# The last block's queries in two halves: even tiles in the first half of the last attention period, odd tiles in the second

## The chip, the core and the metric

The program runs on one core of one Trainium2 chip. The metric is the device time of one execution in microseconds (us); lower is better. Four engines do the arithmetic: TensorE (PE, matrix multiplies; its weight loads are shown as PEld), VectorE (DVE), ScalarE (ACT) and GpSimd (POOL). SyncE (SP) issues the DMA transfers. Each engine runs its own list of instructions strictly in order, and waits for semaphores that others raise.

## What is computed

The input `x` is (4, 64, 64, 64) float32, the output (4, 4096, 64). The three layers, cut to what matters here:

```python
# token layer: a 3x3 filter whose taps are computed per pixel
y = relu(batchnorm(conv1_w @ x)); wdyn = conv2_w @ y + conv2_b
h = sum_k(patches_k(x) * wdyn_k).reshape(b, 4096, 64)
# attention over 4096 tokens, one head of width 64
n = layernorm(h); Q, K, V = n @ Wq + bq, n @ Wk + bk, n @ Wv + bv
h = h + softmax(Q @ K.T / 8) @ V
# feed-forward: each token goes to the best of 32 experts with 16 hidden units each
n = layernorm(h); e = argmax(n @ router_w.T + router_b)
h = h + relu(relu(n @ W1[e] + b1[e]) @ W2[e] + b2[e])
```

## The kernel before

**Blocks.** The 4 x 4096 tokens are worked on in 16 blocks of 1024 queries (`BLOCKS`, numbered 0 to 15); four blocks make one image. A block has 8 tiles of 128 tokens (`BT`), laid out for TensorE as two halves of 512 columns. The keys of an image are 32 tiles, taken as 16 pairs (`PAIRS`).

**Periods.** The program is a list of periods. Period n has 16 groups g = 0 to 15, and in each of them TensorE computes the scores of one pair of key tiles against all 1024 queries of block n (`usual_score`, line 689) and then adds the previous group's exponentials times the keys into the sum `z_ps` (`usual_weigh`, `into_z`, line 700). ScalarE takes the exponentials in between (line 912) into a ring of four buffers. Period 16 has no attention left: it is the tail, in which only the stages of the last block run.

**Stages.** Between score and weighing a group may have "fills", small stages of other blocks, named `name@block`. For a finished block they are, in order: `z` (VectorE adds the two halves of `z_ps` into `z_sb`, lines 1109 and 1111; TensorE may not begin the next sum in `z_ps` before, semaphore `z_copied`); `pz` (TensorE projects to values, line 626; VectorE divides by the softmax sum, adds the residual and normalises, lines 1175 to 1181 and 1010 to 1038, result `y_block`); `yt` (turned by TensorE, line 547, copied to `y_t` by ScalarE, line 889); `lg` (router logits, line 635, copied by ScalarE, line 897; VectorE picks the expert, lines 1053 to 1063, result `onehot`); `ot` (turned, line 547, copied to `onehot_t`, line 900); `hid0` to `hid3` (first expert layer, line 656); `o2` (second layer, lines 663 and 671; its two halves added into `o2_sb`, lines 863 and 1191); `fin` (turned back, line 679; VectorE adds, line 1197, and SP stores the block, line 362).

**Experts.** In blocks 3 to 13 (`CHOSEN_BY_DMA`) the choice of the expert is spread by DMA and VectorE applies it (line 1143). In the others TensorE adds a mask of large negative numbers first (line 652, bf16) and ScalarE takes the relu (line 904); for the last block ScalarE and VectorE take half of it each (lines 904 and 1149, semaphore `upper_hidden`).

**Places.** A fill's result goes to a place in PSUM. The usual one is `both` (place 0), of which there is one, so a fill waits until the fill before it has been read. Once attention is over, the banks of `scores` and `z_ps` are free as well: table `AT_THE_END` spreads the last stages over them (places 7 and 8 are the two banks pairs of `scores`, 9 is `z_ps`).

**What sets the order.** The tables of groups: `usual_groups(n)` puts, in period n, the stages of block n-1 (`pz` at group 2, `yt` 5, `lg` 6, `ot` 8, `hid0` to `hid3` 12 to 15, `o2` 16, `fin` at group 1 of the period after). For block 14 the last two are missing from period 15, because `last_groups` puts `hid0@14` to `hid3@14` and `o2@14` into the tail, behind `pz@15`. Every engine walks through the same tables. In blocks 0 and 1 (n < 2) the attention goes another way, in halves; that part is not touched.

Of the kernel before, what the change touches and what calls it, by code (L numbers as in the profile page):

```python
# [8 lines left out]
ALU = mybir.AluOpType  # L9
# [8 lines left out]
D = W  # L18
HH = 2
# [49 lines left out]
CHOSEN_BY_DMA = range(3, BLOCKS - 2)  # L69
USUAL, FIRST_TAP, TAP_PLACES = 0, 1, 6  # L70
# [10 lines left out]
def at(i, names):  # L81
    return [f"{n}@{i}" for n in names.split()] if 0 <= i < BLOCKS else []
# [120 lines left out]
def vit_block_kernel(nc, x, once, kept, out):  # L203
# [6 lines left out]
    with ExitStack() as ctx:  # L210
# [64 lines left out]
        centred, squares = tap_product[:, 0], tap_product[:, 1]  # L275
# [1056 lines left out]
```

## Time and profile before

| | us |
|---|---|
| three timed runs | 1128.85, 1130.23, 1126.38 (median 1128.85) |
| the profiled execution, its own time | 1131.35 |
| its span in the trace | 1129.3 |
| TensorE busy | 1091.9 (97% of the span) |
| ScalarE busy | 584.1 (52%) |
| VectorE busy | 545.5 (48%) |
| last weighing (line 700) to the end of the span | 35.6 |

The page of the profile gives the busy share of each engine in 40 slices of 28 us. TensorE stands at 9 (90% or more) in all slices except the first and the last. The row of its granted clock stands at 9 (full speed) in most slices and at 8 in the last. The timeline lists instructions in order of time, merged, with the idle time of the engine before them and what released it; a matmul of float32 counts as two instructions in the trace (and as one in the listings of the order below). Four 64x64 matmuls run side by side, so the starts of a row's instructions lie closer together than one of them lasts.

### The profile page before, as it was taken

How to read it: one execution, taken by the hardware profiler on the slowest of the kernel's cores; microseconds unless marked ns; L12 is line 12 of the kernel's file. 1: busy time of each engine (PE TensorE's matmuls, PEld its weight loads, DVE VectorE, ACT ScalarE, POOL GpSimd, SP SyncE). 2: the span in 40 equal slices, each digit the busy share in tenths (PEclk: the TensorE clock that was granted, in tenths of full speed). 3: DMA queues.
4: the chain of work that ended last, by engine and by line, in shares of the span. 5: the costliest groups of instructions: out<-in, count | busy, mean ns of one | idle time of the engine just before them, and what ended most of it. 6: DMA issues, size and time to landing. Idle time of an engine off the chain costs nothing.

```text
span 1129.3 us, 28862 instructions
## 1 busy us (share of the span) xinstructions
PE 1091.9 (97%) x12458; PEld 520.4 (46%) x12458; DVE 545.5 (48%) x1145; ACT 584.1 (52%) x654; POOL 10.7 (1%) x35
## 2 busy tenths in 40 slices
PE   6699999999999999999999999999999999999995
PEld 2233333445444554445544455544545555555542
DVE  6788766428056472645637264553523131412323
ACT  2356666555555464555546455464545455454552
POOL 3000000000000000000000000000000000000000
PEclk9989999999999999999999999999999999999998
DMA  5645612122025131232412123140100101010000
GB/s 152 144 112 127 150 38 61 34 45 61 16 70 117 39 87 23 69 77 61 86 39 82 26 69 78 40 105 10 42 11 11 41 11 41 11 42 10 2 1 20
DMA packets 22385, 63.86 MB, mean 57 GB/s; under 512 B 3550, under 2 KB 7454, under 8 KB 21868
## 3 DMA queue, kind: packets, MB, share of 16 engines
q1 hardware_dynamic: 22252, 61.93, 22.8%
q8 instruction: 102, 1.67, 0.7%
q14 instruction: 31, 0.25, 0.1%
HBM read 53.31 MB, written 5.47 MB: 52 GB/s over the span
## 4 chain that ended last, share of the span: by engine, by line
PE 89%; DVE 5%; issue 2%; DMA 1%; ACT 1%; DVEq 1%; SPq 0%; ACTq 0%
PE z_ps L700 37%; PE scores L689 35%; PE both L656 4%; PE both L671 4%; PE both L547 2%; DMA filter_ring<-filters 1%; PE both L679 1%; PE both L595 1%; PE both L585 1%; PE both L616 1%; DVEq L1004 1%; PE both L626 1%; PE both L635 0%; ACT probs L912 0%; PE both L663 0%
## 5 line engine op out<-in xcount | busy, mean ns | idle before, releaser
L912 ACT ACTIVATE probs<-scores 128x1024 f32<-128x1024 f32 x504 | 488.7, 1021 | 462.2 <-PE scores L689 462.2
L689 PE MATMUL scores<-g_t,keys_t 64*64 64x512 f32 x4096 | 511.0, 593 | 3.0 <-ACT g_t L891 1.2
L700 PE MATMUL z_ps<-probs,keys 64*64 64x512 f32 x4096 | 505.8, 591 | 0.7 <-issue 0.7
L689 PEld LDWEIGHTS scores<-g_t,keys_t 64*64 64x64 f32 x4096 | 206.7, 134 | 242.3 <-issue 235.3
L700 PEld LDWEIGHTS z_ps<-probs,keys 64*64 64x64 f32 x4096 | 193.4, 133 | 193.5 <-issue 183.6
L1143 DVE SCALAR_TENSOR_TENSOR hidden<-both,chosen 128x1024 f32<-128x1024 f32 x44 | 53.9, 1224 | 198.9 <-PE both L656 193.9
L1079 DVE TENSOR_TENSOR hres<-hres,tap_product 128x504 f32<-128x504 f32 (+1 forms) x128 | 88.8, 694 | 10.5
L1074 DVE SCALAR_TENSOR_TENSOR tap_product<-filter_ring,w,xin 128x504 f32<-128x504 f32 (+1 forms) x120 | 89.0, 742 | 6.2 <-DMA filter_ring<-filters 2.9
L656 PE MATMUL both<-y_t,w 64*64 64x512 f32 x464 | 63.4, 597 | 0.0
L671 PE MATMUL both<-hidden,w 64*64 64x512 f32 x448 | 56.6, 592 | 0.0
L1187 DVE COPY o_sb<-both 128x512 f32<-128x512 f32 x14 | 9.7, 691 | 82.9 <-PE both L671 82.9
L1109 DVE COPY z_sb<-z_ps 128x512 f32<-128x512 f32 x14 | 9.7, 692 | 69.6 <-PE z_ps L700 69.6
L656 PEld LDWEIGHTS both<-y_t,w 64*64 64x64 f32 x464 | 22.6, 134 | 24.5 <-issue 23.9
L1053 DVE TENSOR_REDUCE stat<-logits 128x8 f32<-128x256 f32 x16 | 6.7, 419 | 55.4 <-ACT logits L897 55.4
L671 PEld LDWEIGHTS both<-hidden,w 64*64 64x64 f32 x448 | 23.8, 133 | 20.7 <-issue 19.8
L1175 DVE RECIPROCAL stat<-both 128x8 f32<-128x8 f32 x16 | 3.3, 208 | 57.4 <-PE both L626 57.4
L1029 DVE TENSOR_TENSOR tap_product<-tap_product 128x512 f32<-128x512 f32 x32 | 22.2, 692 | 2.7 <-issue 0.4
L1031 DVE TENSOR_REDUCE stat<-tap_product 128x8 f32<-128x512 f32 x32 | 22.0, 686 | 2.3
L547 PE MATMUL both<-w,keys 64*64 64x64 f32 x512 | 11.8, 232 | 10.5 <-DVE keys L1038 10.3
L547 PEld LDWEIGHTS both<-w,keys 64*64 64x64 f32 x512 | 11.3, 145 | 21.7 <-issue 21.7
L1015 DVE SCALAR_TENSOR_TENSOR stat<-stat 128x8 f32<-128x8 f32 x96 | 16.1, 167 | 7.9 <-issue 0.9
L1019 DVE SCALAR_TENSOR_TENSOR stat<-stat 128x8 f32<-128x8 f32 x96 | 16.1, 167 | 7.8 <-issue 0.9
(138 smaller groups left out, 552.8 us busy)
## 6 DMA issues: line engine op xcount, KB each, us to landing
filter_ring<-filters SPq DMA_DIRECT2D x90, 384.0 KB, 5.2
chosen<-choices SPq DMA_DIRECT2D x44, 256.0 KB
out_dram<-out_sb SPq DMA_DIRECT2D x32, 128.0 KB, 2.6
xin<-x_dram SPq DMA_DIRECT2D x6, 528.0 KB, 9.1
g_t<-g_t SPq DMA_DIRECT2D x24, 128.0 KB, 5.6
hidden<-once_dram SPq DMA_DIRECT2D x1, 930.0 KB, 12.5
choices<-onehot_t SPq DMA_DIRECT2D x22, 32.0 KB, 1.6
hidden<-once_dram SPq DMA_DIRECT2D x1, 576.0 KB, 4.6
```

Of the source, the lines that this page charges most:

```text
L547: last = T.matmul(both[rows_of(a), h, j * 64:(j + 1) * 64], tiles[2 * j + a][rows_of(h)], ident[rows_of(h), rows_of(h)], start=True, stop= ...
L656: last = T.matmul(mine[rows_of(c), r, :], w1[rows_of(r), cols[c]], y_t[rows_of(r), :], start=i in CHOSEN_BY_DMA, stop=True)
L671: last = T.matmul(mine[rows_of(r), h, :], w2[rows_of(h), f, :], hidden[rows_of(h), f, r, :], start=(f == 0 and h != r), stop=(f == FT - 1))
L689: last = T.matmul(scores[rows_of(h), c, r * 512:(r + 1) * 512], keys_t[rows_of(r), i // NQ % 2, k * 128 + 64 * h:k * 128 + 64 * h + 64], g ...
L700: last = T.matmul(z_ps[rows_of(c), h, :], keys[rows_of(h), i // NQ % 2, 2 * k + r, :], probs[rows_of(h), (2 * g + c) % RING, r * 512:(r + ...
L912: A.activation(probs[:, unit % RING, :], scores[:, c, :], ACT.Exp, scale=first_scale[:, 0:1] if n == 0 and g <= ASKED else SCALE).then_inc ...
L1015: V.scalar_tensor_tensor(half, dst, -0.5, dst, ALU.mult, ALU.mult)
L1029: V.tensor_tensor(squares[:, :, :], centred[:, :, :], centred[:, :, :], ALU.mult)
L1031: V.reduce_sum(total, squares[:, :, :], AX_X)
L1074: product = V.scalar_tensor_tensor(dst, flt, keep["b2c"][:, t:t + 1], pix, ALU.add, ALU.mult)
L1079: V.tensor_tensor(mine[:, :, lo:hi], mine[:, :, lo:hi], dst, ALU.add)
L1143: V.scalar_tensor_tensor(hidden[:, f, :, :], place[k][:, :, :], 0.0, chosen[:, f, :, :], ALU.max, ALU.mult).then_inc(drained[k], 1)
```

## The change

The last block (15) becomes two parts. Part `EVEN` (number 15) holds its tiles 0, 2, 4, 6, part `ODD` (number 16) its tiles 1, 3, 5, 7, 512 queries each. In period 15 the first 8 groups work on all 32 key tiles for the even queries, the second 8 groups on all of them for the odd queries: a group takes two pairs of key tiles against one half of the queries, where it took one pair against both halves. Number and shape of the score and weighing matmuls stay.

The stages of `EVEN` then run inside period 15, from its group 8 on (`z`, `pz`, `yt`, `lg`, `ot`), and its `hid`, `o2`, `fin` in the tail; those of `ODD` all run in the tail. Block 14's `hid0` to `hid3` and `o2` move from the tail into period 15, its `fin` stands in the tail. Stages of a part are half as wide (256 columns in place of 512), `pz` apart, whose TensorE part keeps its size. Each part is stored by itself, 64 partitions x 4 tiles of 256 bytes in each of two DMAs, in place of 64 partitions x 2048 bytes.

```diff
-AT_THE_END = {f"{name}@{BLOCKS - 2}": k for name, k in (("hid0", 7), ("hid1", 8), ("hid2", 7), ("hid3", 8), ("o2", 9))}
-AT_THE_END |= {f"{name}@{BLOCKS - 1}": k for name, k in (("hid1", 7), ("hid2", 8), ("o2", 9))}
+AT_THE_END = {f"fin@{EVEN - 1}": 7, f"fin@{EVEN}": 9}
+AT_THE_END |= {f"{name}@{EVEN}": k for name, k in (("hid0", 8), ("hid1", 9), ("hid2", 8), ("hid3", 9), ("o2", 8))}
+AT_THE_END |= {f"{name}@{ODD}": k for name, k in (("hid1", 7), ("hid2", 8), ("o2", 9))}
...
-def attention(n, g):
-
-    if n > 1:
-        return n, g
-    return g // HALF, n * HALF + g % HALF
+def attention(n, g, c):
+
+    if n < 2:
+        return g // HALF, n * HALF + g % HALF, c
+    if n == BLOCKS - 1:
+        return n, g % HALF * 2 + c, g // HALF
+    return n, g, c
...
+def halved_groups():
+
+    m = EVEN - 1
+    return merged(usual_groups(BLOCKS - 1),
+                  {HALF: at(EVEN, "z"), 9: at(m, "hid0"), 10: at(EVEN, "pz"), 11: at(m, "hid1"), 12: at(m, "hid2"),
+                   13: [*at(m, "hid3"), *at(EVEN, "yt")], 14: at(EVEN, "lg"), 15: at(m, "o2"), 16: at(EVEN, "ot")})
...
-    m = BLOCKS - 1
-    return merged({-1: at(m, "z"), 2: at(m, "pz"), 3: at(m - 1, "hid0 hid1 hid2 hid3 o2"), 5: at(m, "yt"), 6: at(m, "lg"),
-                   7: at(m - 1, "fin"), 8: at(m, "ot"), 9: at(m, "hid0 hid1 hid2 hid3"), 15: at(m, "o2"),
-                   16: at(m, "fin")})
+    return merged({-1: at(ODD, "z"), 1: at(EVEN - 1, "fin"), 2: at(ODD, "pz"), 3: at(EVEN, "hid0 hid1 hid2 hid3 o2"),
+                   5: at(ODD, "yt"), 6: at(ODD, "lg"), 7: at(EVEN, "fin"), 8: at(ODD, "ot"),
+                   9: at(ODD, "hid0 hid1 hid2 hid3"), 15: at(ODD, "o2"), 16: at(ODD, "fin")})
...
+                    if m < EVEN:
+                        rows, mine = (v.rearrange("c t w -> c (t w)") for v in (rows, mine))
+                    else:
+                        rows = rows.rearrange("c (j a) w -> c a j w", a=2)[:, m - EVEN]
+                    sp.dma_start(rows, mine).then_inc(out_stored[m % 2], 16)
...
-                        pe.wait_ge(z_copied, n)
+                        pe.wait_ge(z_copied, n + (g > 0))
...
+            def half_block(i, sums, done):
+
+                tiles = residual(EVEN).rearrange("p (j a) w -> p a j w", a=2)[:, i - EVEN]
+                whole = tap_product[:, :, :, :].rearrange("p k t w -> p (k t w)")[:, 0:BT // 2 * 65]
+                whole = whole.rearrange("p (j w) -> p j w", w=65)
+                rs, mine = stat[:, 4, 0:BT // 2], h2[:, i % 2, 0:BT // 2, :]
+                settle()
+                V.tensor_copy(whole, sums[:, 0])
+                settle()
+                V.tensor_tensor(whole, whole, sums[:, 1], ALU.add).then_inc(done, 1)
+                settle()
+                V.reciprocal(rs, whole[:, :, D])
+                settle()
+                V.tensor_tensor(mine, whole[:, :, 0:D], wide(rs, D), ALU.mult)
+                settle()
+                V.tensor_tensor(mine, mine, tiles, ALU.add)
+                settle()
+                normalise(mine)
+                write_normalised(y_block[:, 0:BT // 2, :]).then_inc(y_ready, 1)
```

**Order on TensorE at the end of period 15, before:** attention runs undisturbed to its last two weighings (x16), and `pz@15` and `hid0@14` follow.

```order
L689 MATMUL scores<-g_t,keys_t 64x512 x8
L700 MATMUL z_ps<-probs,keys 64x512 x16
L626 MATMUL both<-wv_w,z_sb 64x65 x16
L652 MATMUL scores<-onehot_t,mask_w 64x512 x4
L656 MATMUL scores<-y_t,w 64x512 x4
```

**The same place after** (groups 13 to 16; line 726 is the score, 737 the weighing, 687 and 692 `hid3@14`, 581 `yt@EVEN` and then `ot@EVEN`, 668 `lg@EVEN`, 700 and 708 `o2@14`):

```order
L687 MATMUL both<-onehot_t,mask_w 64x512 x4
L692 MATMUL both<-y_t,w 64x512 x4
L581 MATMUL both<-w,y_block 64x64 x8
L737 MATMUL z_ps<-probs,keys 64x512 x8
L726 MATMUL scores<-g_t,keys_t 64x512 x8
L668 MATMUL both<-router_w,y_t 64x32 x8
L737 MATMUL z_ps<-probs,keys 64x512 x8
L726 MATMUL scores<-g_t,keys_t 64x512 x8
L700 MATMUL both<-onehot_t,b_parts 64x512 x4
L708 MATMUL both<-hidden,w 64x512 x16
L737 MATMUL z_ps<-probs,keys 64x512 x8
L581 MATMUL both<-ident_bf,onehot 64x64 x8
```

Block 14's expert layers and four small stages of `EVEN` now stand between score and weighing of period 15, and `hid3@14` and `yt@EVEN` stand next to each other in the same place `both`.

**Order on TensorE in the tail, before** (from the last of `hid3@14`: `o2@14`, `yt@15`, `lg@15`, `fin@14`, `ot@15`, `hid0@15`):

```order
L656 MATMUL scores<-y_t,w 64x512 x4
L663 MATMUL z_ps<-onehot_t,b_parts 64x512 x4
L671 MATMUL z_ps<-hidden,w 64x512 x16
L547 MATMUL both<-w,y_block 64x64 x16
L635 MATMUL both<-router_w,y_t 64x32 x16
L679 MATMUL both<-w,o_sb 64x64 x16
L547 MATMUL both<-ident_bf,onehot 64x64 x16
L652 MATMUL both<-onehot_t,mask_w 64x512 x4
L656 MATMUL both<-y_t,w 64x512 x4
```

**The same place after** (from the last of `hid3@EVEN`: `o2@EVEN`, `yt@ODD`, `lg@ODD`, `fin@EVEN`, `ot@ODD`, `hid0@ODD`):

```order
L692 MATMUL z_ps<-y_t,w 64x256 x4
L700 MATMUL scores<-onehot_t,b_parts 64x256 x4
L708 MATMUL scores<-hidden,w 64x256 x16
L581 MATMUL both<-w,y_block 64x64 x8
L668 MATMUL both<-router_w,y_t 64x32 x8
L716 MATMUL z_ps<-w,o_sb 64x64 x8
L581 MATMUL both<-ident_bf,onehot 64x64 x8
L687 MATMUL both<-onehot_t,mask_w 64x256 x4
L692 MATMUL both<-y_t,w 64x256 x4
```

The same stages in the same order, each at half its columns or half its count; `fin` now has a place of its own (`z_ps`), so `ot` need not wait until VectorE has read it.

**Order on VectorE between the last sum and the normalising, before:**

```order
L1109 COPY z_sb<-z_ps 128x512
L1111 TENSOR_TENSOR z_sb<-z_sb,z_ps 128x512
L1175 RECIPROCAL stat<-both 128x8
L1178 TENSOR_TENSOR h<-both,stat 128x4x64 x2
L1181 TENSOR_TENSOR h<-h,hres 128x512
L1025 TENSOR_REDUCE stat<-h 128x8
```

**After, for `ODD`** (line 1265 is `fin@14`):

```order
L1171 COPY z_sb<-z_ps 128x512
L1173 TENSOR_TENSOR z_sb<-z_sb,z_ps 128x512
L1265 SCALAR_TENSOR_TENSOR out_sb<-scores,h 128x4x64 x2
L1130 COPY tap_product<-both 128x260
L1132 TENSOR_TENSOR tap_product<-tap_product,both 128x260
L1134 RECIPROCAL stat<-tap_product 128x4
L1136 TENSOR_TENSOR h<-tap_product,stat 128x256
L1138 TENSOR_TENSOR h<-h,hres 128x256
L1065 TENSOR_REDUCE stat<-h 128x4
```

A copy and a sum are new (the two halves of the keys meet only here), the two multiplies became one, the widths are halved, and `fin@14` stands ahead.

## Rows read from the trace of the kernel before

**Rows 1.** Timeline, TensorE, period 15: start us, us, engine, line, operation, count.
```profile
1042.10 1.99 PE L689 MATMUL scores<-g_t,keys_t 64*64 64x512 f32 x16
...
1046.01 1.98 PE L689 MATMUL scores<-g_t,keys_t 64*64 64x512 f32 x16
...
1049.44 1.98 PE L689 MATMUL scores<-g_t,keys_t 64*64 64x512 f32 x16
```

**Rows 2.** Timeline, TensorE, stage o2@13 and the score behind it.
```profile
1030.96 0.38 PE L663 MATMUL both<-onehot_t,b_parts 64*64 64x512 bf16 x1
...
1034.45 2.30 PE L689 MATMUL scores<-g_t,keys_t 64*64 64x512 f32 x16
```

**Rows 3.** Timeline, TensorE, tail; in brackets idle time before and releaser.
```profile
1095.83 0.43 PE L652 MATMUL scores<-onehot_t,mask_w 64*64 64x512 bf16 x4
...
1096.91 0.42 PE L652 MATMUL scores<-onehot_t,mask_w 64*64 64x512 bf16 x4
...
1104.80 0.69 PE L547 MATMUL both<-w,y_block 64*64 64x64 f32 x32 [0.34 <-DVE y_block L1038]
...
1110.88 0.43 PE L547 MATMUL both<-ident_bf,onehot 64*64 64x64 bf16 x16 [2.75 <-DVE out_sb L1197]
1112.09 0.64 PE L652 MATMUL both<-onehot_t,mask_w 64*64 64x512 bf16 x4 [0.79 <-ACT onehot_t L900]
```

**Rows 4.** Timeline, VectorE, tail.
```profile
1093.75 0.69 DVE L1109 COPY z_sb<-z_ps 128x512 f32<-128x512 f32 x1 [30.83 <-PE z_ps L700]
...
1096.10 0.21 DVE L1175 RECIPROCAL stat<-both 128x8 f32<-128x8 f32 x1 [0.90 <-PE both L626]
...
1097.23 0.69 DVE L1181 TENSOR_TENSOR h<-h,hres 128x512 f32<-128x512 f32 x1
1097.99 0.69 DVE L1025 TENSOR_REDUCE stat<-h 128x8 f32<-128x512 f32 x1
...
1101.05 0.17 DVE L1033 TENSOR_SCALAR stat<-stat 128x8 f32<-128x8 f32 x1
...
1103.97 0.68 DVE L1038 TENSOR_TENSOR y_block<-tap_product,stat 128x504 f32<-128x504 f32 x1
...
1107.41 0.42 DVE L1053 TENSOR_REDUCE stat<-logits 128x8 f32<-128x256 f32 x1 [1.50 <-ACT logits L897]
1107.91 0.42 DVE L1055 TENSOR_TENSOR pick<-logits,stat 128x256 f32<-128x256 f32 x1
...
1124.66 0.76 DVE L1197 SCALAR_TENSOR_TENSOR out_sb<-both,h 128x256 f32<-128x256 f32 x2 [0.90 <-PE both L679]
```

**Rows 5.** Timeline, ScalarE, period 15 and tail.
```profile
1054.03 1.94 ACT L912 ACTIVATE probs<-scores 128x1024 f32<-128x1024 f32 x2 [1.49 <-PE scores L689]
1055.86 0.59 ACT L889 COPY y_t<-both 128x512 f32<-128x512 f32 x1
...
1097.17 2.10 ACT L904 ACTIVATE hidden<-scores 128x1024 f32<-128x1024 f32 x2 [5.78 <-PE scores L656]
...
1107.01 0.37 ACT L897 COPY logits<-both 128x256 f32<-128x256 f32 x1 [0.87 <-PE both L635]
...
1122.39 0.59 ACT L863 COPY o_sb<-z_ps 128x512 f32<-128x512 f32 x1 [3.27 <-PE z_ps L671]
```

**Rows 6.** Windows: stretch, length, busy per engine, TensorE's granted clock, DMA share, GB/s.
```profile
64.00:65.00 1.00, 1.00 (x12) 0.26 (x8) 0.91 (x2) 0.84 (x1) 0.00 (x0) 0.70 0.20 37
...
1109.00:1110.00 1.00, 0.00 (x0) 0.00 (x0) 0.93 (x3) 0.00 (x0) 0.00 (x0) 0.54 0.00 0
...
1115.00:1116.00 1.00, 1.00 (x8) 0.21 (x4) 0.19 (x1) 0.10 (x1) 0.00 (x0) 0.54 0.00 0
```

**Rows 7.** Timeline, TensorE, the earlier stretch at half clock.
```profile
58.69 3.69 PE L689 MATMUL scores<-g_t,keys_t 64*64 64x512 f32 x16 [0.69 <-ACT keys_t L887]
```

**Rows 8.** DMAs: landing of the 32 block stores (line 362); page, the filter loads' median.
```profile
DMA to landing us min/median/max: 2.3/2.6/3.6
...
filter_ring<-filters SPq DMA_DIRECT2D x90, 384.0 KB, 5.2
```

More of the change, by code:

```diff
@@ L432, in _ @@
             copy_queries(NQ)
-            for n in range(1, BLOCKS + 2):
+            for n in range(1, PARTS + 2):
                 if n > 1 and n % NQ == 1 and n // NQ + 2 < B:
@@ L542, in turn @@
             def turn(tiles, ident=ident):
-                for j in range(BT // 2):
+                for j in range(len(tiles) // 2):
                     for h in range(2):
@@ L631, in fill @@
                     wait_drained(f"yt@{i}")
-                    for j in range(BT // 2):
+                    for j in range(half_tiles(i)):
                         for r in range(2):
@@ L640, in fill @@
                     pe.wait_ge(onehot_ready, i + 1)
-                    last = turn([onehot[:, t, :, :].rearrange("p u e -> p (u e)") for t in range(BT)], ident_bf)
+                    last = turn([onehot[:, t, :, :].rearrange("p u e -> p (u e)") for t in range(2 * half_tiles(i))],
+                                ident_bf)
                     last.then_inc(done, 1)
@@ L645, in fill @@
                     wait_drained(f"ot@{i}")
-                    if i == BLOCKS - 1 and f == FT - 1:
+                    if i == ODD and f == FT - 1:
                         pe.wait_ge(upper_hidden, 1)
                     cols = [slice(f * 128 + 64 * c, f * 128 + 64 * c + 64) for c in range(2)]
+                    tokens = slice(0, width(i))
                     for r in range(2):
@@ L675, in fill @@
                     wait_drained(f"o2@{i}")
-                    for j in range(4):
+                    for j in range(half_tiles(i)):
                         for r in range(2):
                             for h in range(2):
-                                last = T.matmul(both[rows_of(h), r, j * 64:(j + 1) * 64],
+                                last = T.matmul(mine[rows_of(h), r, j * 64:(j + 1) * 64],
                                                 o2_sb[rows_of(r), j * 128 + h * 64:j * 128 + h * 64 + 64],
@@ L859, in drain @@
                     A.copy(a_w[:, :], z_ps[:, 1, 0:128]).then_inc(a_ready, 1)
-                if name == "o2" and i >= BLOCKS - 2:
+                if name == "o2" and i >= EVEN - 1:
                     k = places.of[full]
                     act.wait_ge(filled[k], places.nth[full])
-                    A.copy(o2_sb[:, :], place[k][:, 0, :]).then_inc(lower_copied, 1)
+                    A.copy(o2_sb[:, 0:width(i)], place[k][:, 0, 0:width(i)]).then_inc(lower_copied, 1)
                 if name.startswith(NONE) or not name.startswith(MINE):
@@ L888, in drain @@
                 elif name == "yt":
-                    A.copy(in_order(y_t[:, :]), turned).then_inc(done, 1)
+                    A.copy(in_order(y_t[:, 0:width(i)]), turned).then_inc(done, 1)
                 elif name == "g" and i < NQ:
@@ L1020, in rsqrt @@
                     settle()
-            total, var, scratch, rstd = (stat[:, k, :] for k in range(4))
             def normalise(src):
+                n = src.shape[1]
+                total, var, scratch, rstd = (stat[:, k, 0:n] for k in range(4))
+                centred, squares = (tap_product[:, k, 0:n] for k in range(2))
                 V.reduce_sum(total, src, AX_X)
@@ L1145, in drain @@
                     return
-                if name.startswith("hid") and i == BLOCKS - 1:
+                if name.startswith("hid") and i == ODD:
                     f, k = int(name[3:]), places.of[full]
                     dve.wait_ge(filled[k], places.nth[full])
-                    V.tensor_scalar(hidden[:, f, 1, :], place[k][:, 1, :], 0.0, None, ALU.max).then_inc(upper_hidden, 1)
+                    V.tensor_scalar(hidden[:, f, 1, 0:width(i)], place[k][:, 1, 0:width(i)], 0.0, None,
+                                    ALU.max).then_inc(upper_hidden, 1)
                     return
```

113 lines of the change are left out of this document (66 added, 47 removed).

## The prediction

> **What bounds the kernel now.** I read the page first: TensorE is busy for 97% of the span and has no free slice between the first and the last, so an instruction added to a period costs its full length, and only the ends hold idle time. Then the timeline of TensorE. In period 15 a group without a stage takes 1049.44 - 1046.01 = 3.43 us from score to score, without a gap [rows 1]. Then the tail, engine by engine [rows 3 to 5]: VectorE picks up the last sum at 1093.75 and the span ends at 1129.3, 35.55 us later. It is one chain that goes from engine to engine: VectorE makes `y_block` (to 1103.97 + 0.68 = 1104.65), and TensorE uses that time for `hid@14` and `o2@14`, which it leaves just before `yt@15` starts at 1104.80 after 0.34 us of idleness [rows 3, 4]. Both therefore end at about the same time. From there to the end everything lies on the path. The windows show TensorE's granted clock fall from 2.4 to 1.2 GHz inside 1109 to 1110 and rise inside 1115 to 1116 [rows 6].
>
> **What the period gains: about 10.3 us.** (1) `hid0@14` to `hid3@14`: one is 1096.91 - 1095.83 = 1.08 us with its mask [rows 3], four are 4.3. (2) `o2@14`: the same stage of block 13 takes 1034.45 - 1030.96 = 3.49 [rows 2]. (3) `pz@EVEN` keeps its size on TensorE: a group with `pz` is 1046.01 - 1042.10 = 3.91 us, so 0.48 more than an empty one [rows 1]. `yt` and `lg` have the same count of matmuls at full width and half the count here, 0.24 each; `ot`, bf16, 0.1. Together 1.06. (4) A wait is new. `yt@EVEN` stands behind `hid3@14`, in the same group and the same place `both`, and ScalarE reads `hid3@14` only behind the group's two exponentials. ScalarE's pair starts 1.16 us after the score does (1054.03 against a score start at 1046.01 + 2 x 3.43 = 1052.87) and what follows it starts 1.83 later (1055.86) [rows 1, 5], so 2.99 after the score's start; the relu of 1024 columns is half of 2.10, and 0.14 passes until TensorE goes on (y_block's end at 1104.65 to 1104.80): 4.18. TensorE is done with `hid3` at 1.72 + 1.08 = 2.80 (score, stage). It stands for 1.38 us, and the weighing, the next scores and all that follows stand with it. (5) `ot@EVEN` waits until VectorE has added `o2@14` in `both`. ScalarE's copy (0.59) and VectorE's sum (0.69) with their hand-overs take about as long as the weighing between them (1.72): 0.1. Sum 4.3 + 3.49 + 1.06 + 1.38 + 0.1 = 10.3; the last sum is ready at 1104.05.
>
> **What costs nothing there.** The new `z@EVEN`: TensorE may start the odd queries' sum only after VectorE's 1.5 us of `z`. Between the two weighings stand a score (1.72) and `hid0@14` (1.08) [rows 1, 3], 2.8 against about 1.8 with hand-overs; without `hid0` there it would be 0.1 us. VectorE is free then, its row of 1093.75 says idle for 30.83 us [rows 4]. The single place `both` between `hid0`, `pz`, `hid1`, `hid2`: each next stage stands a whole group later (3.4 us), its reader needs 1.05 behind the exponentials. Had yt stood in group 14, (4) would be gone too. The score matmuls keep number and shape. SP issues nothing new in the period.
>
> **What the tail loses.** Widths halve, fixed costs stay. From start to start VectorE needs 1097.99 - 1097.23 = 0.76 for 512 elements and 1107.91 - 1107.41 = 0.50 for 256; 12 small ones take 1103.97 - 1101.05 = 2.92 [rows 4]. By the same slope 128 elements are 0.36.
> - `z` and `pz`: 1096.10 - 1093.75 = 2.35, unchanged. `fin@14` (0.76) is taken while `pz` runs.
> - to `y_block`: 8 steps of 256 (the new copy and sum among them) 4.0, reciprocal 0.26, small ones 2.92, the last 0.42: 7.6 (before 1104.65 - 1096.10 = 8.55). `hid@EVEN` and `o2@EVEN`, half of 4.3 + 3.49 = 3.9 plus some waits for ScalarE's two places, end at about 7 and are hidden; if that cover were gone, they would cost 3.9.
> - to `ot`: before 1110.88 - 1104.65 = 6.23 [rows 3, 4], of which 0.72 is `fin@14` on VectorE in front of `ot` (the releaser of `ot@15`); it now has its own place. The two matmul stages 0.69 to 0.45 each, ScalarE 0.59 to 0.37 and 0.37 to 0.27 [rows 5], picks 4 x 0.50 to 4 x 0.36, `onehot` 0.76 to 0.5: 4.1.
> - `ot` to `hid0`: 1112.09 - 1110.88 = 1.21 becomes 0.85.
> - `hid` and `o2` of the last part: before 1122.39 - 1112.09 = 10.3 [rows 3, 5]. At full clock half of it is 2.15 + 1.75 and about 0.35 until the result: 4.25. The clock fell at 1109.08 (0.92 us of that window at half) and rose at 1115.92, 3.8 us after `hid0@15` began; at 60 us it rose at 64.6, 5.9 after the dense work of 58.69 [rows 6, 7]. Half of this time is lost. Taking the middle, 4.9: 2.45. Together 6.7.
> - to the last result: before 1124.66 + 0.76 - 1122.39 = 3.03; ScalarE, VectorE twice and a transpose narrower by 0.22 + 0.27 + 0.26 + 0.23: 2.05.
> - the store: before 1129.3 - 1125.42 = 3.9. Half the bytes, but 256 pieces of 256 bytes in place of 64 of 2048. The nearest row is the same store, landing in 2.3 to 3.6, median 2.6; the farthest in this direction the filter loads with 192 pieces, 5.2 [rows 8]. So -0.3 to +2.6; I take +0.3, near the store's own row, since 64 KB is little: 4.2.
> Sum 2.35 + 7.6 + 4.1 + 0.85 + 6.7 + 2.05 + 4.2 = 27.85, which is 7.7 less than 35.55.
>
> The net is 10.3 - 7.7 = +2.6 us. Why halving the tail's work does not pay: of the 7.8 us of `hid@14` and `o2@14` nearly all was hidden below VectorE's chain, and in the period nothing hides it. The trace of before ends at 1129.3, so after it 1131.9; the profiled execution (1131.35) lies 2.5 above the median of the runs, so I put the difference on the median: 1128.85 + 2.6 = 1131.4.
>
> **A rule against the store.** The profile's 32 stores all write pieces of 2048 bytes, and no row prices smaller ones to memory [rows 8]. The Trainium skill (DMA: Bandwidth & Descriptors, Specifications) says that full rate wants at least 512 bytes per piece and that below this the DMA engine reads, modifies and writes. No run here shows it. The rival "small pieces" has its price from the rows alone.
>
> **Rivals.** A measurement of this kernel tells 0.3% (3.4 us) from no change.
> - *The clock stays low to the end* (slower). TensorE has less to do between `o2@EVEN` and `hid0@ODD` than before: 7 us with four half-sized bursts. If the clock falls earlier, those bursts take up to 0.2 longer each (0.6), and if it does not rise before `o2@ODD` is over, all of 4.25 is doubled but for the hand-over: 3.9 in place of 2.45 lost. Sum +4.65: 1133.5. It decides when the rise comes later than about 6.5 us after `hid0@ODD`. For it: 5.9 in rows 6 and 7. Against: 3.8 in the tail itself. 0.20.
> - *Small pieces.* The last store lands like the filter loads, 5.2 in place of 2.6: +2.3 on the forecast, 1133.7. 0.08.
> - *The clock does not fall.* Idle stretches on TensorE are shorter than the 2.8 us before `ot@15`; the loss of 2.45 goes: +0.15, 1129.0. Against: less work in all than before, and it fell then. 0.10.
> - *The halves don't separate*: the choice for `EVEN` is not there when TensorE reaches `ot@EVEN`, which stands in front of the last weighing. VectorE has it about 5 us before by my count (`lg` two groups ahead, pick 2 us). If missed, each us is paid in full; 2 us give 1133.4. 0.03.
> - *The period takes less*, because the added stages find gaps that the modelled matmul ends hide, by 6 us or more: below 1125.5. TensorE's 3.43 us per group is 32 instructions at 0.107 without a gap, so hardly. 0.05.
>
> **How the numbers follow.** Forecast 1131.4 with 0.54. The range takes in the clock that does not fall at its lower end (1129.0, less 0.8 for the spread of the runs) and both slower rivals at the upper (1133.7 and a little): 1128.2 to 1134.2. Slower by over 0.3% begins at 1132.2: the two or three slower rivals give 0.31. Faster: 0.05. Within: 0.64.
>
> **What would show it.** In the profile after: the last sum's copy on VectorE at about 1104; one idle stretch of TensorE of 1.3 us in front of `yt@EVEN`, released by ScalarE's relu; `y_block` 7.6 us after `pz@ODD`; TensorE idle about 3 us before `yt@ODD`; half clock over `hid@ODD`. I am wrong if the copy comes well before 1103 (the period is cheaper) or if from there to the end it is less than 26 or more than 30 us.

## The result and the profile after

| | before | after |
|---|---|---|
| median of twelve runs, us | 1128.97 | 1133.32 |
| lowest, highest | 1126.32, 1131.52 | 1130.77, 1134.44 |
| ratio, 95% interval | | 1.003 [1.0021, 1.004] |
| the profiled execution, its own time | 1131.35 | 1132.14 |
| its span in the trace | 1129.3 | 1130.1 |

The changed kernel is slower: by 4.35 us between the medians, by 3.4 us as a ratio. The forecast was 1131.4 with a range of 1128.2 to 1134.2, so the time lies inside the range and 1.9 above the forecast, and the effect lies on the 0.3% line that was to part "no change" from "slower". Both kernels were measured once more (y1 and y2 below), which gave 1.0021 [1.0012, 1.003] for the changed one and 0.999 [0.9978, 1.0002] for the old one. Over both measurements the change costs about 2.9 us.

Two marks make the traces comparable. **M** is the start of TensorE's second score group behind `o2@13` (the group after the one at 1034.45 in [rows 2]), 1037.89 before and 1037.29 after. Up to M both kernels issue instructions of the same kind, shape and order. **Z** is the start of VectorE's last copy of the sum, 1093.75 before [rows 4]. Z - M is what period 15 and its neighbourhood take, span - Z is the tail.

The timeline of TensorE around the score at M, and at the place where period 15 of the changed kernel differs most (start us, us, engine, line, operation, count; in brackets idle time before and releaser):

```profile
1037.29 2.30 PE L726 MATMUL scores<-g_t,keys_t 64*64 64x512 f32 x16
...
1086.26 0.46 PE L687 MATMUL both<-onehot_t,mask_w 64*64 64x512 bf16 x4
1086.47 1.10 PE L692 MATMUL both<-y_t,w 64*64 64x512 f32 x8
1088.69 0.46 PE L581 MATMUL both<-w,y_block 64*64 64x64 f32 x16 [1.11 <-ACT hidden L942]
1088.97 1.90 PE L737 MATMUL z_ps<-probs,keys 64*64 64x512 f32 x16
```

The first two rows after the dots are `hid3@14`, the third is `yt@EVEN`, the last is the weighing behind it. TensorE stands idle in front of `yt@EVEN` for 1.11 us, until ScalarE has read `hid3@14`. ScalarE's timeline shows why it read so late, behind the two exponentials of the group:

```profile
1085.68 1.94 ACT L951 ACTIVATE probs<-scores 128x1024 f32<-128x1024 f32 x2 [1.55 <-PE scores L726]
1087.61 1.02 ACT L942 ACTIVATE hidden<-both 128x1024 f32<-128x1024 f32 x1
1089.22 0.37 ACT L927 COPY y_t<-both 128x256 f32<-128x256 f32 x1 [0.58 <-PE both L581]
```

The tail on VectorE (the rows that answer to [rows 4]):

```profile
1103.71 0.69 DVE L1171 COPY z_sb<-z_ps 128x512 f32<-128x512 f32 x1 [2.15 <-PE z_ps L737]
...
1106.13 0.43 DVE L1130 COPY tap_product<-both 128x260 f32<-128x260 f32 x1 [0.30 <-PE both L659]
...
1113.26 0.42 DVE L1079 TENSOR_TENSOR y_block<-tap_product,stat 128x252 f32<-128x252 f32 x1
...
1126.37 0.49 DVE L1265 SCALAR_TENSOR_TENSOR out_sb<-both,h 128x128 f32<-128x128 f32 x2 [0.66 <-PE both L716]
```

and on TensorE (to [rows 3]), the last four rows being `yt@ODD`, `ot@ODD`, `hid0@ODD` and the transpose of `fin@ODD`:

```profile
1108.96 1.89 PE L708 MATMUL scores<-hidden,w 64*64 64x256 f32 x30
1113.83 0.46 PE L581 MATMUL both<-w,y_block 64*64 64x64 f32 x16 [2.98 <-DVE y_block L1079]
...
1117.75 0.32 PE L581 MATMUL both<-ident_bf,onehot 64*64 64x64 bf16 x8 [2.10 <-DVE onehot L1105]
1118.64 0.43 PE L687 MATMUL both<-onehot_t,mask_w 64*64 64x256 bf16 x4 [0.56 <-ACT onehot_t L938]
...
1125.85 0.46 PE L716 MATMUL both<-w,o_sb 64*64 64x64 f32 x16 [1.11 <-DVE o_sb L1257]
```

VectorE now needs 1113.26 + 0.42 - 1103.71 = 9.97 us to `y_block`, before 10.90 [rows 4]. In those 10 us TensorE has less to do than before and goes idle for 2.98 us, where it was idle for 0.34 [rows 3]. ScalarE's last relevant row is the copy at 1124.81 that ends `o2@ODD`:

```profile
1124.81 0.37 ACT L900 COPY o_sb<-z_ps 128x256 f32<-128x256 f32 x1 [1.56 <-PE z_ps L708]
```

The windows over the tail (columns as in [rows 6]) show where TensorE's granted clock falls from 2.4 to 1.2 GHz and where it comes back:

```profile
1115.00:1116.00 1.00, 0.66 (x32) 0.51 (x30) 0.29 (x1) 0.27 (x1) 0.00 (x0) 0.76 0.08 16
1116.00:1117.00 1.00, 0.00 (x0) 0.00 (x0) 0.84 (x3) 0.00 (x0) 0.00 (x0) 0.50 0.00 0
...
1122.00:1123.00 1.00, 1.00 (x26) 0.80 (x22) 0.56 (x2) 0.52 (x2) 0.00 (x0) 0.83 0.00 0
```

A mean clock of 0.76 over one microsecond is 0.52 us at full and 0.48 us at half, so the clock fell at about 1115.5; 0.83 means in the same way that it rose at about 1122.3. Nearly all of `hid@ODD` therefore runs at half clock, and `o2@ODD` at full clock.

Put together, period and tail of the two kernels in two profiled executions each:

| | M | Z | Z - M | tail | Z - M + tail |
|---|---|---|---|---|---|
| before | 1037.89 | 1093.75 | 55.86 | 35.55 | 91.41 |
| before again (y2) | 1036.70 | 1092.56 | 55.86 | 34.84 | 90.70 |
| after | 1037.29 | 1103.71 | 66.42 | 26.39 | 92.81 |
| after again (y1) | 1037.50 | 1103.92 | 66.42 | 27.58 | 94.00 |

Z - M is 10.56 longer in both pairs, the tail 8.2 shorter on average, so the net is +2.35 on average. M itself moves by more than a microsecond between executions of one kernel. The two single spans, 1129.3 and 1130.1, differ by 0.8 only: the changed kernel reached M 0.60 us earlier there, and its tail was the shorter one of its two.

### The profile page after: what moved, and what is told of

It is laid out like the page before. It is cut to its first block, busy times and chain, and to the rows that moved or that the text cites. A ratio compares the mean times of both kernels' runs of the same rounds, so it can differ in the third digit from the quotient of the medians.

```text
span 1130.1 us, 29180 instructions
## 1 busy us (share of the span) xinstructions
PE 1090.7 (97%) x12574; PEld 524.0 (46%) x12574; DVE 551.6 (49%) x1179; ACT 586.0 (52%) x662; POOL 11.5 (1%) x35
## 4 chain that ended last, share of the span: by engine, by line
PE 89%; DVE 5%; issue 2%; DMA 1%; ACT 1%; DVEq 1%; SPq 0%; ACTq 0%
PE z_ps L737 37%; PE scores L726 35%; PE both L708 5%; PE both L692 5%; PE both L581 2%; DMA filter_ring<-filters 1%; PE both L716 1%; PE both L629 1%; PE both L649 1%; PE both L619 1%; PE both L659 1%; DVEq L1043 1%; ACT probs L951 1%; PE both L668 0%; PE both L700 0%
## 5 line engine op out<-in xcount | busy, mean ns | idle before, releaser
L692 PE MATMUL both<-y_t,w 64*64 64x512 f32 (+1 forms) x496 | 66.8, 587 | 0.0
L708 PE MATMUL both<-hidden,w 64*64 64x512 f32 x480 | 60.7, 592 | 0.0
L1095 DVE TENSOR_REDUCE stat<-logits 128x8 f32<-128x256 f32 (+1 forms) x17 | 6.9, 403 | 67.3 <-ACT logits L935 67.3
L1171 DVE COPY z_sb<-z_ps 128x512 f32<-128x512 f32 x15 | 10.4, 692 | 45.7 <-PE z_ps L737 45.7
L1069 DVE TENSOR_TENSOR tap_product<-tap_product 128x512 f32<-128x512 f32 (+1 forms) x33 | 22.3, 676 | 2.8 <-issue 0.4
L1071 DVE TENSOR_REDUCE stat<-tap_product 128x8 f32<-128x512 f32 (+1 forms) x33 | 22.1, 670 | 2.4
L581 PE MATMUL both<-w,keys 64*64 64x64 f32 x512 | 11.8, 232 | 10.9 <-DVE keys L1079 10.9
L1058 DVE SCALAR_TENSOR_TENSOR stat<-stat 128x8 f32<-128x8 f32 (+1 forms) x99 | 16.6, 167 | 8.4 <-issue 1.3
L1054 DVE SCALAR_TENSOR_TENSOR stat<-stat 128x8 f32<-128x8 f32 (+1 forms) x99 | 16.6, 167 | 8.2 <-issue 0.9
```

Source lines behind the costliest of these rows:

```text
L581: last = T.matmul(both[rows_of(a), h, j * 64:(j + 1) * 64], tiles[2 * j + a][rows_of(h)], ident[rows_of(h), rows_of(h)], start=True, stop= ...
L692: last = T.matmul(mine[rows_of(c), r, tokens], w1[rows_of(r), cols[c]], y_t[rows_of(r), tokens], start=i in CHOSEN_BY_DMA, stop=True)
L708: last = T.matmul(mine[rows_of(r), h, tokens], w2[rows_of(h), f, :], hidden[rows_of(h), f, r, tokens], start=(f == 0 and h != r), stop=(f ...
L1054: V.scalar_tensor_tensor(half, dst, -0.5, dst, ALU.mult, ALU.mult)
L1069: V.tensor_tensor(squares[:, :, :], centred[:, :, :], centred[:, :, :], ALU.mult)
L1071: V.reduce_sum(total, squares[:, :, :], AX_X)
```

## The experiments

Each kernel ran beside the kernel before on the same chip. Ratios are against it, with their 95% interval.

### x1: `yt@EVEN` and the stages behind it one group later

```diff
 def halved_groups():
-    13: [*at(m, "hid3"), *at(EVEN, "yt")], 14: at(EVEN, "lg"), 15: at(m, "o2"), 16: at(EVEN, "ot")})
+    13: at(m, "hid3"), 14: at(EVEN, "yt"), 15: at(EVEN, "lg"), 16: at(m, "o2")})
 def last_groups():
-    return merged({-1: at(ODD, "z"), 1: ...
+    return merged({-1: at(ODD, "z"), 0: at(EVEN, "ot"), 1: ...
```

> The changed kernel with hid3@14 and yt@EVEN in groups of their own: yt@EVEN in group 14, lg@EVEN in 15, o2@14 in 16, ot@EVEN behind the last weighing. Theory (the wait of 1.1 us in front of yt@EVEN is paid in full): that idle row is gone, no other takes its place, the last sum is ready 1.1 to 1.4 us earlier, the time is 1.2 us below the changed kernel, some 3 above the kernel before (ratio 1.0027). Rival (TensorE would have waited elsewhere): no difference to the changed kernel, ratio 1.0038.

Measured: 1.0022 [1.0007, 1.0036], median 1132.35 against 1129.35. Z - M = 64.96, so 1.46 less than in the changed kernel, and the wait has gone from TensorE's timeline:

```profile
1087.04 0.46 PE L687 MATMUL both<-onehot_t,mask_w 64*64 64x512 bf16 x4
1087.25 1.10 PE L692 MATMUL both<-y_t,w 64*64 64x512 f32 x8
1088.11 1.96 PE L737 MATMUL z_ps<-probs,keys 64*64 64x512 f32 x16
1089.83 1.96 PE L726 MATMUL scores<-g_t,keys_t 64*64 64x512 f32 x16
1091.54 0.43 PE L581 MATMUL both<-w,y_block 64*64 64x64 f32 x15
1091.78 0.60 PE L737 MATMUL z_ps<-probs,keys 64*64 64x512 f32 x2
```

The mechanism of the wait is shown, and its price in the period. Counted from start to start, `hid3@14` alone takes 1088.11 - 1087.04 = 1.07 us here and `yt@EVEN` alone 1091.78 - 1091.54 = 0.24, where in the changed kernel the two with the wait take 1088.97 - 1086.26 = 2.71. The wait is therefore 1.40 us; the idle row says 1.11, because the ends of matmuls are modelled. The rest of the 1.46 is `ot@EVEN`, which x1 moves behind the last weighing and so out of Z - M (0.08). In the timed runs the gain can't be told from nothing. The tail was 27.27 here: the clock was at half from about 1112.6 to 1122.9. So the trace alone says 92.23 for period and tail, against 92.81 and 94.00.

### x2: only block 14's stages moved, nothing split

```diff
-AT_THE_END = {f"{name}@{BLOCKS - 2}": k for name, k in (("hid0", 7), ...
-    if m in CHOSEN_BY_DMA:
+    if m in CHOSEN_BY_DMA or m == BLOCKS - 2:
         return merged(groups, {12: at(m, "hid0"), 13: at(m, "hid1"), ..., 16: at(m, "o2")})
 def last_groups():
-    2: at(m, "pz"), 3: at(m - 1, "hid0 hid1 hid2 hid3 o2"), 5: ...
+    2: at(m, "pz"), 5: ...
```

> The kernel before, with nothing split, and only hid0@14 to hid3@14 and o2@14 moved from the tail into groups 12 to 16 of period 15. Theory (7.8 us of work that VectorE's chain hid is laid bare): the last sum is ready 7.8 us later, the tail from there stays at 35 to 36 us, or 1 to 2 us more if the clock now falls earlier for want of that work: 7.8 to 9.8 us above the kernel before, ratio 1.007 to 1.009. Rival (this work was on the tail's path, and moving it shortens the tail): under 3 us above.

Measured: 1.0085 [1.0067, 1.0104], median 1139.28 against 1129.35. Z - M = 64.02, 8.16 more than before, and the tail did not get shorter at all: 36.57. TensorE's timeline shows the hole that block 14 leaves under VectorE's chain:

```profile
1102.83 0.70 PE L625 MATMUL both<-wv_w,z_sb 64*64 64x65 f32 x32 [1.64 <-DVE z_sb L1110]
1112.62 1.13 PE L546 MATMUL both<-w,y_block 64*64 64x64 f32 x32 [9.09 <-DVE y_block L1037]
```

The windows show the clock falling inside that hole (0.87 over this microsecond, so at about 1104.7):

```profile
1104.00:1105.00 1.00, 0.00 (x0) 0.00 (x0) 0.91 (x3) 0.00 (x0) 0.00 (x0) 0.87 0.00 0
```

With the half clock in place already at `yt@15`, that stage takes 1.13 us in place of 0.69. This is the run that carries the explanation: the move of block 14 alone costs 9.6 us by the ratio, 9.5 by the traces. All its stages are paid in full in the period (8.16), and the tail gets 1.0 to 1.7 us longer in place of shorter, with the clock at half from the hole until about 1125.2.

### x3: only the split, block 14 stays where it was

`halved_groups` loses `hid` and `o2` of block 14, `last_groups` keeps them, and `EVEN` and `ODD` get places and columns of `y_t`, `onehot_t` and `hidden` of their own, so that `EVEN`'s stages can wait until later than `ODD`'s first ones. So x3 differs from the changed kernel in two things: block 14 stays in the tail, and `EVEN`'s stages there stand elsewhere (`hid` in front of `ot@ODD`, `o2` and `fin` between the stages of `ODD`).

```diff
 def halved_groups():
+    {HALF: at(EVEN, "z"), 10: at(EVEN, "pz"), 13: at(EVEN, "yt"), 14: at(EVEN, "lg"), 16: at(EVEN, "ot")})
 def last_groups():
+    m = EVEN - 1
+    return merged({-1: at(ODD, "z"), 0: at(m, "hid0"), 2: at(ODD, "pz"), 3: at(m, "hid1 hid2 hid3 o2"),
+                   5: at(ODD, "yt"), 6: at(ODD, "lg"), 7: at(EVEN, "hid0 hid1 hid2 hid3"), 8: at(ODD, "ot"),
+                   9: at(m, "fin"), 10: at(ODD, "hid0 hid1"), 11: at(EVEN, "o2"), 12: at(ODD, "hid2 hid3"),
+                   14: at(EVEN, "fin"), 15: at(ODD, "o2"), 16: at(ODD, "fin")})
```

> The changed kernel, the last block split as there, but block 14's hid0 to hid3 and o2 back in the tail, below VectorE's chain for ODD (hid0@14 in the gap of z@ODD), as in the kernel before; EVEN's hid0 to hid3 go between lg@ODD and ot@ODD where TensorE idles, its o2 and fin between the stages of ODD. The parts get y and one-hot tiles and columns of the hidden tile of their own. Theory (the price of the change is the 7.8 us of block 14 laid bare, the split itself is a gain): period 15 grows by 1 us only, the tail is 26 to 28 us, 7 to 9 shorter than before's 35.5, and with TensorE busy the clock falls later or not at all: 5 to 8 us below the kernel before, ratio 0.993 to 0.996. Rival (the work put back only fills the gaps that the split won, or delays ODD's chain): within 2 us of the kernel before.

Measured: 0.9929 [0.9916, 0.9943], median of five runs 1122.59 against 1129.27. It beats both kernels: 8.0 us below the one before as a ratio, 6.7 between the medians. Z - M = 56.89, 1.03 above before. The tail is 27.29, as long as the changed kernel's, though it holds the 7.8 us of block 14 as well. TensorE's timeline of the tail:

```profile
1100.94 3.60 PE L723 MATMUL z_ps<-hidden,w 64*64 64x512 f32 x30
1105.03 0.46 PE L596 MATMUL both<-w,y_block 64*64 64x64 f32 x16 [0.49 <-DVE y_block L1094]
1106.07 0.43 PE L683 MATMUL both<-router_w,y_last 64*64 64x32 f32 x16 [0.57 <-ACT y_last L942]
1106.29 0.32 PE L702 MATMUL scores<-onehot_last,mask_w 64*64 64x256 bf16 x4
...
1108.95 0.26 PE L596 MATMUL both<-ident_bf,onehot 64*64 64x64 bf16 x8
```

The granted clock in the windows (columns as in [rows 6]) at three places of the tail:

```profile
1105.00:1106.00 1.00, 0.46 (x16) 0.35 (x16) 0.69 (x1) 0.58 (x2) 0.00 (x0) 1.00 0.00 0
1109.00:1110.00 1.00, 0.79 (x44) 0.65 (x40) 0.16 (x1) 0.97 (x3) 0.00 (x0) 1.00 0.00 0
1114.00:1115.00 1.00, 0.99 (x33) 0.61 (x30) 1.00 (x4) 0.69 (x2) 0.00 (x0) 1.00 0.00 0
```

Block 14 again fills the 10 us to `y_block`; TensorE waits 0.49 us there in place of 2.98, and `EVEN`'s hidden stages fill the wait in front of `ot@ODD`. The granted clock does not fall in the tail until all matrix work is over (0.86 over 1119 to 1120). The stages from `hid0@ODD` to ScalarE's copy take 1116.87 - 1110.11 = 6.76 us here, because `EVEN`'s `o2` stands among them; in the changed kernel half clock brought the same stretch to 6.17 and 7.03.

Part of the gain is the clock: against the kernel before with its clock kept up (x7 below, 0.9983) x3 is 6.1 us faster by the ratios and 4.7 by the traces. How much of that the split alone would give, with `EVEN`'s stages where the changed kernel has them, no run separates.

### x4: `fin@14` of the kernel before in a place of its own

```diff
-("o2", 9))}
+("o2", 9), ("fin", 8))}
...
```

The lines left out make `fin` write to that place and VectorE read it there.

> The kernel before, with fin@14 in a place of its own (place 8), nothing else. Theory (ot@15 waited for VectorE's two sums of fin@14, 0.72 us): ot@15 starts 0.7 us earlier after the pick, tail 34.8 in place of 35.5, time 0.7 us below the kernel before, ratio 0.9994. Rival (ScalarE or the clock sets it): no difference.

Measured: 1.0003 [0.9992, 1.0014]. No effect is to be seen, but the 0.9994 that was expected lies in the interval too. The trace shows that `ot@15` did come 5.65 us behind `y_block` in place of 6.23, a gain of 0.58. The tail was 35.22, between the 35.55 and 34.84 of the kernel before. In this execution the gain was lost again to the clock: it rose at about 1114.7, 5.3 us after `hid0@15` began, where in the kernel before it rose 3.8 us after it [rows 3, 6]. The stretch at half clock was as long as there, 6.8 us, but began later, 16.2 us after Z (0.95 over 1107 to 1108) in place of 15.3 and 15.0. Whether the edit moved it or chance did, one trace can't say. TensorE's `ot@15`, now released by the choice itself, and `hid0@15`:

```profile
1108.24 0.43 PE L547 MATMUL both<-ident_bf,onehot 64*64 64x64 bf16 x16 [2.86 <-DVE onehot L1063]
1109.45 0.64 PE L652 MATMUL both<-onehot_t,mask_w 64*64 64x512 bf16 x4 [0.78 <-ACT onehot_t L900]
```

The window in which the clock rose:

```profile
1114.00:1115.00 1.00, 1.00 (x12) 0.40 (x8) 0.69 (x1) 0.59 (x1) 0.00 (x0) 0.63 0.00 0
```

### x6: the changed kernel with its idle gaps filled by unread matmuls

```diff
+    if full == f"yt@{ODD}":
+        wait_drained(f"fin@{EVEN - 1}")
+        keep_busy(14)
+    if full == f"ot@{ODD}":
+        keep_busy(8)
```

`keep_busy(n)` issues n score matmuls into the free banks of `scores`, and nobody reads them.

> The changed kernel with 14 matmuls more in front of yt@ODD and 8 more in front of ot@ODD, whose results nobody reads, to keep TensorE busy where it idles. Theory (hid@ODD and part of o2@ODD at half clock cost 1.9 us): granted clock stays at 1.0 over the tail, ot@ODD to the result of o2@ODD is 2 us shorter, time 2 us below the changed kernel (ratio 1.0020 to the kernel before). Rival (the clock falls anyway, or the matmuls delay the stages behind them): no gain, up to 1 us loss.

Measured: 1.0007 [0.9995, 1.0019], median 1130.32 against 1129.35; tail 24.78. Against the changed kernel's 1.003 and 1.0021 that is 2.6 and 1.6 us less (the interval of the first is clear of x6's, that of the second overlaps it); in the traces the tail is 1.6 and 2.8 us shorter. The clock stays at full speed, and a quarter of `hid@ODD` takes 0.54 us in place of 1.04 to 1.07. TensorE's timeline, the first row being the unread matmuls in front of `ot@ODD`:

```profile
1114.61 1.93 PE L589 MATMUL scores<-g_t,keys_t 64*64 64x512 f32 x16
1117.01 0.26 PE L581 MATMUL both<-ident_bf,onehot 64*64 64x64 bf16 x8 [0.47 <-DVE onehot L1117]
1117.83 0.30 PE L699 MATMUL both<-onehot_t,mask_w 64*64 64x256 bf16 x4 [0.56 <-ACT onehot_t L950]
...
1118.37 0.30 PE L699 MATMUL scores<-onehot_t,mask_w 64*64 64x256 bf16 x4
```

From `hid0@ODD` to ScalarE's copy it is 1122.18 - 1117.83 = 4.35 us, where the changed kernel took 6.17 and 7.03. So half clock costs it 1.8 and 2.7 us in this stretch.

### x7: the same in the kernel before

```diff
+    if full == f"ot@{BLOCKS - 1}":
+        keep_busy(10)
```

> The kernel before, with 10 matmuls whose result nobody reads in front of ot@15, where TensorE idles 2.75 us and the clock falls. Theory (the half clock costs 1.9 to 3 us in the tail of before as well): the clock stays at 1.0, time 2 us below the kernel before, ratio 0.998. Rival (the clock falls later instead, over hid@15, or before the matmuls): no difference.

Measured: 0.9983 [0.9974, 0.9992], median 1128.02 against 1129.27; tail 32.98 against 35.55 and 34.84. The kernel before pays about the same toll to the clock, 1.9 us, so the clock is not what parts the two kernels: with it kept up in both (x6 against x7) the change still costs 2.7 us by the ratios and 91.20 - 88.84 = 2.36 by the traces.

### x8: x1 and x6 together

> The changed kernel with both edits: hid3@14 and yt@EVEN in groups of their own, and the unread matmuls in front of yt@ODD and ot@ODD. Theory (the wait of 1.1 us, of which 0.7 arrives at the last sum, and the clock's 2 to 3 us are separate and add up): ratio to the kernel before 1.0000, 3.5 us below the changed kernel. Rival (they overlap): no better than with the matmuls alone, 1.0007.

Measured: 0.999 [0.9981, 0.9999], median 1129.28 against 1129.27. Z - M = 64.96 and a tail of 24.76, 89.72 together, 1.48 less than x6. The wait's price shows in the traces again. In the timed runs 1.0007 falls to 0.999, but the two intervals overlap by 0.0004, so there it stands at the edge of what the runs resolve. Even with both faults mended the changed kernel only reaches the kernel before, and is no faster than x7 (0.9983).

### x5: the store in pieces of 1024 bytes

The parts take the tiles 0 to 3 and 4 to 7 in the output, where they hold the even and the odd ones: the tiles of the last block are exchanged, and the pieces are four times as long.

```diff
-    rows = rows.rearrange("c (j a) w -> c a j w", a=2)[:, m - EVEN]
+    rows = rows.rearrange("c (a j) w -> c a j w", a=2)[:, m - EVEN]
+    rows, mine = (v.rearrange("c t w -> c (t w)") for v in (rows, mine))
```

> The changed kernel, with the two parts of the last block stored in pieces of 1024 bytes in place of 256: each part's four tiles go to four places that lie next to each other, which are not their own (the tiles of the last block are exchanged in the output, all else is computed as before). Theory (small pieces cost nothing at 64 KB): from VectorE's last instruction to the end of the span 3.2 to 3.4 us, as with pieces of 256 bytes. Rival (pieces below 512 bytes are slower): 0.3 us or more shorter than with 256 bytes.

Measured, in one execution: 1131.59 us. From the end of VectorE's last row (1126.06 + 0.49) to the end of the span (1129.6) it is 3.05 us. With pieces of 256 bytes the same stretch was 3.24 and 3.30 in the changed kernel and in between in x1, x3, x6 and x8; with 2048 bytes and twice the data it was 3.88 in the first trace of the kernel before and 3.31 to 3.40 in y2, x2, x4 and x7. So 3.05 is less than either expectation had: below the 3.2 to 3.4 of "pieces cost nothing", and short of the 0.3 us that the rival wanted. Small pieces may cost about 0.2 us, which rests on a single execution; they do not cost 2. The last row of VectorE:

```profile
1126.06 0.49 DVE L1266 SCALAR_TENSOR_TENSOR out_sb<-both,h 128x128 f32<-128x128 f32 x2 [0.67 <-PE both L717]
```

### y1 and y2: both kernels once more

> The changed kernel itself once more, with another trace. From the score behind o2@13 (in period 15's neighbourhood, the mark M) to the last sum it took 66.42 us before and 66.42 is expected again, and the tail behind it 26.4, give or take 1 for where the clock falls. Theory (the difference between the traces, +1.4 us, and between the timed runs, +3.4, comes from when M is reached, which moves by 2 us from execution to execution for reasons of the opening): M between 1035 and 1038.5, ratio 1.002 to 1.004. Rival (the change makes the tail slower in most executions than in the one profiled): tail over 27.5 us in this trace.

> The kernel before itself once more, with another trace: M to the last sum 55.86 us again, tail 35 to 35.6 (the store 3.3 to 3.4 us in place of the first trace's 3.9), M anywhere from 1033 to 1038.5, ratio 1.000. Rival: the tail of the first trace was a long one and is under 34.5 here.

Measured: 1.0021 [1.0012, 1.003], median 1132.75, for the changed kernel, and 0.999 [0.9978, 1.0002], 1129.61, for the kernel before, against 1130.11 on that chip. Z - M came out the same to 0.01 us (66.42 and 55.86). The changed kernel's tail was 27.58, over the 27.4 of the theory and just over the 27.5 from which the rival counts, so the first trace's 26.39 was on the short side (x5, with the same order, had 26.35). The reason is the clock, which fell earlier (at about 1114.3) and rose later (at about 1124.6) than in the first trace, 10.2 us at half in place of 6.8, as the windows have it:

```profile
1114.00:1115.00 1.00, 0.52 (x16) 0.36 (x16) 0.23 (x1) 0.37 (x1) 0.00 (x0) 0.66 0.00 0
1124.00:1125.00 1.00, 1.00 (x19) 0.71 (x16) 0.10 (x1) 0.05 (x1) 0.00 (x0) 0.72 0.00 0
```

The kernel before had a tail of 34.84, between the 35 of the theory and the 34.5 of its rival. Its store took 3.33 us in place of 3.88, which is most of the 0.7 to the first trace.

## Why the prediction was right, step by step

**The period.** The three larger terms were measured apart. What x2 adds is block 14, what x3 adds is the small stages, what x1 takes away is the wait:

| term | forecast | measured |
|---|---|---|
| `hid@14` and `o2@14` in the period | 7.8 | 8.16 (x2) |
| `EVEN`'s `pz`, `yt`, `lg`, `ot` | 1.06 | 1.03 (x3) |
| wait in front of `yt@EVEN` | 1.38 | 1.46 (x1), of which the wait is 1.40 |
| `o2@14` in front of `ot@EVEN` | 0.1 | -0.1 (what is left; no wait in the trace) |
| sum | 10.3 | 10.56 |

The largest term is 0.4 too small. The four `hid` stages cost the 1.08 us each that the prediction gave them (1.07 in x1). `o2@14` takes 3.49 us to the next weighing, as forecast, but in the changed kernel the weighing behind it takes 2.06 us to the next start (1099.56 to 1101.62) in place of 1.72. The row that the prediction read for `o2@13` ends at the next start and can't show that. The three edits add up, 8.16 + 1.03 + 1.46 = 10.65 against 10.56 together. That is what one expects where a single engine is full, and the one wait found was the only one.

**The tail.**

| stretch | forecast | after | after again |
|---|---|---|---|
| last sum to `y_block`'s end | 9.95 | 9.97 | 9.98 |
| to `ot@ODD` | 4.1 | 4.07 | 4.34 |
| to `hid0@ODD` | 0.85 | 0.89 | 0.88 |
| to ScalarE's copy behind `o2@ODD` | 6.7 | 6.17 | 7.03 |
| to the last result | 2.05 | 2.05 | 2.05 |
| the store, to the end of the span | 4.2 | 3.24 | 3.30 |
| sum | 27.85 | 26.39 | 27.58 |

The slope of VectorE's time over the width (0.76, 0.50, 0.36 for 512, 256, 128 elements) carried the stretch to `y_block` to within 0.03 us. The 4.1 to `ot@ODD` fits the traces better than its own working does: what the prediction takes off 6.23 leaves 3.9, since it counts 0.72 for `fin@14`, and x4 showed 0.58. The mis-sized term is the store, by 0.9. It started from the 3.9 of the one trace at hand, which was a long one (3.33 when the same kernel was profiled again), and 0.3 was added for small pieces, where x5 leaves room for 0.2 at most. In the difference 0.5 of this cancels, since the old store was as much too long in the sum it was subtracted from; 0.4 stays. The loss to half clock was put at 2.45, and it was 1.8 and 2.7: the middle of the two rows was about right, and the traces lie on either side of it.

**The net.** Forecast +2.6. The two pairs of traces give +2.35, the timed runs +3.4 and +2.4. That the sum came so close is partly luck: the period was put 0.26 too low and the tail's saving 0.5 too low, and the two errors work against each other. Something lies outside the span as well: the difference between an execution's time and its span was 2.57 and 2.31 on average for the changed kernel, 2.06 for the kernel before. These 0.3 to 0.5 us bring traces and times together (2.35 + 0.4 against 2.9), but what they are is not settled. x1 (2.37) and x3 (2.43) have them too, x6 (1.97) and x8 (2.02) do not, although these issue the same transfers.

**The reason given.** "In the period nothing hides it" is shown by x2 and x3 together: the move costs 9.6 us alone, and the split without it, in x3's order, wins 8.0 by the ratio (6.7 between the medians). Together that makes +1.6, and the wait in front of `yt@EVEN`, which only the two edits together bring, adds 1.4: 3.0, where 2.9 was measured. The prediction did see that block 14's work had been hidden, and priced `EVEN`'s cover correctly. What it never asked is whether the split needs the move. Its loss was in the pairing of the two edits, and the profile of before had the answer: 0.34 us of idleness in front of `yt@15` [rows 3] says that block 14 fitted where it stood.

**The rivals.**
- *The clock stays low to the end.* Not as named: it rose 3.7 us after `hid0@ODD` began (first trace) and 5.4 us after it (second), both before the 6.5 from which the rival would decide. But its ingredient is real. Counted from Z, the clock fell after 15.3 us in the kernel before (15.0 in y2, 16.2 in x4), and after 11.8, 12.1 (x5), 10.4 (y1), 9.6 (x1) and 3.5 us (x2) where TensorE had been given less cover work. It stayed at half for 6.8 us in the first trace and 10.2 in y1 and x1. Filling the gaps was worth 1.6 to 2.6 us in the changed kernel (x6), 1.9 in the kernel before (x7).
- *Small pieces.* Refuted at its price by the traces and by x5: 3.24 and 3.30 us against 3.05. The Trainium skill (DMA: Bandwidth & Descriptors, Specifications) says that pieces below 512 bytes are read, modified and written. In these transfers of 64 KB at most 0.2 us of that can be seen; had it the price that the rival gave it, 2.3 us, the stretch would have been over 5.
- *The clock does not fall.* It fell in both traces.
- *The halves don't separate.* They do: nothing waits in front of `ot@EVEN` at 1101.62.
- *The period takes less.* It took 0.26 more.

**The chances.** "Within 0.3%" had 0.64 and "slower" 0.31; the first measurement came out at the line itself (1.003) and the second below it (1.0021). The forecast's 0.23% was sound, and the chance for slower, which began 0.8 above the forecast, was set too low, since two measurements of the same pair differ by 1.0 us.

## What to carry to other kernels

Block 14's work lay under another engine's chain and cost nothing there; moved into a phase where its own engine is full it cost 9.6 us. Before moving such work, look for the idle row that it fills (0.34 us here with it, 9.09 without it). Splitting the last block is worth 7 to 8 us in this kernel when the covering work stays in the tail and the first part's own stages fill what gaps remain, and some 2 of these are the clock. Make the two edits apart first: together they showed +0.3% and hid one of -0.7% and one of +0.85%.

## What the runs showed of the hardware

- The same instruction stream took the same time to 0.01 us from M to Z in every profiled execution (55.86 in the four of before, y2, x4 and x7, 66.42 in the four of after, y1, x5 and x6), while M itself lay anywhere between 1033.56 and 1038.07. Most of the scatter of this kernel's times comes from ahead of period 15 (4.5 us in M against 0.7 and 1.2 in the tails), and a difference of two single spans says little.
- When TensorE's granted clock falls and rises differs between executions of one kernel: after 11.8 and 10.4 us from Z in the changed kernel, for 6.8 and 10.2 us, which made 1.2 us in the tail. An edit that wins less than that, like x4's 0.58, can't be read from one trace. Only where the gaps were filled, with real work in x3 or unread matmuls in x6, x7 and x8, did the clock stay at 2.4 GHz until the matrix work was over, worth 1.9 us in x7.
- The last store, two transfers of 128 KB in 2048-byte pieces, took 3.31 to 3.88 us from the last result to the end of the span (five traces); two of 64 KB took 3.24 to 3.30 in 256-byte pieces (six traces), and 3.05 in 1024-byte ones (one trace). Half the bytes saved hardly 0.1 us against the usual 3.31 to 3.40.
